# Attention operands kept in three parts per head, a re-ordered first pair of heads, and unread products on TensorE at three stage borders

## The reference, cut to what matters

```python
x = _layernorm(x + attn0(x))    # 16 heads of 8, causal, ALiBi-like decay -|i-j|
x = _layernorm(x + moe(x))      # 8 experts, top 1, 128 -> 512 -> 128
x = _layernorm(x + attn1(x))    # 16 heads of 64, q and k RMS-normalised, gated decay
x = _layernorm(x + ffn(x))      # 128 -> 512 -> 512 -> 512 -> 128
```

## Time and profile before

| | us |
|---|---|
| median of 3 runs | 2205.83 |
| lowest and highest run | 2204.80 and 2212.89 |
| profiled execution, its own time | 2213.37 |
| span of the profile | 2211.6 |
| PE busy | 2041.5 |
| DVE busy | 1389.9 |
| ACT busy | 1146.0 |
| POOL busy | 839.6 |

### The profile page before, as it was taken

The page is one execution under the profiler, slowest core; times in us unless marked ns, Lnnn a source line. Parts: engine busy times, 40 slices in busy tenths (PEclk is TensorE's granted clock), DMA queues, the critical chain, the costliest instruction groups (busy, mean ns, idle before and its releaser), DMA issues.

```text
span 2211.6 us, 37667 instructions
## 1 busy us (share of the span) xinstructions
PE 2041.5 (92%) x13392; PEld 1231.1 (56%) x13392; DVE 1389.9 (63%) x3316; ACT 1146.0 (52%) x1859; POOL 839.6 (38%) x544
## 2 busy tenths in 40 slices
PE   5799999998487988896999999999999999999998
PEld 3355455554476544454566666666666665656644
DVE  4788888883632787874677777777777764333311
ACT  2366666666344676782455555555555552232232
POOL 5000000001501445442577777777777772000000
PEclk8799999999589999995899999999999999999999
DMA  5233333113165689897477677767776697433300
GB/s 177 104 128 133 134 130 119 59 54 98 65 188 151 187 268 338 270 287 181 105 180 180 154 177 180 182 161 173 178 182 166 168 223 211 110 86 86 91 5 10
DMA packets 260313, 336.09 MB, mean 152 GB/s; under 512 B 22732, under 2 KB 181756, under 8 KB 259720
## 3 DMA queue, kind: packets, MB, share of 16 engines
q1 hardware_dynamic: 244824, 305.82, 51.6%
q0 software_dynamic: 7664, 24.39, 3.1%
q10 hardware_dynamic: 7640, 3.48, 0.6%
HBM read 193.69 MB, written 122.62 MB: 143 GB/s over the span
## 4 chain that ended last, share of the span: by engine, by line
PE 49%; DMA 2%; SPq 2%; DVE 0%; ACT 0%; issue 0%; DVEq 0%
PE ps L959 11%; PE ps L1296 10%; PE ps L910 7%; PE ps L941 6%; PE ps L942 6%; PE ps L1247 2%; PE ps L947 1%; PE ps L1307 1%; PE ps L922 1%; PE ps L1284 1%; PE ps L1285 1%; SPq L1171 1%; DMA a1QA<-a1QB 1%; DMA a1FQ<-s_q 1%; DMA s_y<-a1raw 0%; DMA fyb<-s_y 0%
## 5 line engine op out<-in xcount | busy, mean ns | idle before, releaser
L1132 POOL TENSOR_TENSOR a1sum<-a1sum,a1prob 128x1024 f32<-128x1024 f32 (+3 forms) x256 | 461.3, 1802 | 101.7 <-ACT a1prob L1075 69.7
L1075 ACT ACTIVATE a1prob<-ps 128x512 f32<-128x512 f32 (+2 forms) x640 | 322.7, 555 | 239.1 <-PE ps L947 206.3
L480 DVE TENSOR_REDUCE a0grid<-ps 128x8 f32<-128x1024 f32 x288 | 346.6, 1222 | 99.4 <-PE ps L350 48.8
L581 ACT ACTIVATE a0prob<-ps 128x1024 f32<-128x1024 f32 x288 | 291.3, 1027 | 159.0 <-PE ps L376 89.2
L1011 DVE CUSTOM_DVE_ANT_0 ps<-ps,c_mask_ij 128x128 f32<-128x128 f32 x496 | 264.6, 551 | 92.0 <-issue 87.7
L959 PE MATMUL ps<-a1prob,a1V 128*64 128x512 f32 (+3 forms) x1536 | 275.5, 501 | 4.9 <-ACT a1prob L1075 4.9
L941 PE MATMUL ps<-a1QA,a1KA 69*128 69x512 f32 (+3 forms) x768 | 272.3, 362 | 4.0 <-DMA a1QA<-a1neg 4.0
L942 PE MATMUL ps<-a1QB,a1KB 128*128 128x512 f32 (+3 forms) x768 | 264.9, 353 | 0.0
L910 PE MATMUL ps<-a1KA,a1QA 68*128 68x128 f32 x744 | 229.4, 385 | 5.0 <-DMA a1KA<-s_g 4.3
L959 PEld LDWEIGHTS ps<-a1prob,a1V 128*64 128x64 f32 x1536 | 103.3, 139 | 174.4 <-issue 140.2
L1014 DVE TENSOR_REDUCE a1mx<-ps 128x1 f32<-128x320 f32 x248 | 146.0, 589 | 60.0 <-PE ps L910 57.2
(11 more groups left out here) (269 smaller groups left out, 3191.7 us busy)
## 6 DMA issues: line engine op xcount, KB each, us to landing
a1FQ<-s_q SPq DMA_DIRECT2D x128, 256.0 KB, 7.8
a1KB<-s_k SPq DMA_DIRECT2D x128, 256.0 KB, 8.6
s_xs<-c_zero POOLq DMA_DIRECT2D x19, 1024.0 KB, 8.9
s_q<-mqkT SPq DMA_DIRECT2D x32, 512.0 KB, 4.0
s_v<-mv SPq DMA_DIRECT2D x32, 512.0 KB, 5.8
s_k<-a1KH SPq DMA_DIRECT2D x32, 512.0 KB, 4.9
s_k<-a1KL SPq DMA_DIRECT2D x32, 512.0 KB, 5.9
a1KA<-s_k SPq DMA_DIRECT2D x64, 256.0 KB
```

The source lines that it names most:

```text
L480: dve.tensor_reduce(grid[g % 2][:, :, a:b + 1:b - a], banks(("max", k)), axis=AX.X, op=ALU.max).then_inc(s1_free, 1)
L581: act.activation(prob[:, :, a:b + 1:b - a, :], banks(("exp", q)), ACT.Exp).then_inc(p_full, 1)
L1075: act.activation(weights_of(g, u)[:, group[0]:group[-1] + 1, off:BANK], both(e, u, group), ACT.Exp).then_inc(weighed, 1)
L1132: pool.tensor_tensor(t[:, :, off:BANK], t[:, :, off:BANK], weights_of(g, u)[:, :, off:BANK], ALU.add).then_inc(summed, 1)
```

## The change

Scratch q0 and k0 hold three parts per head in neighbouring rows (high, high, low for q; high, low, high for k). `store` makes six transfers of 256 KB per chunk instead of four. K and Q of a group are then loaded by two transfers of 48 rows, BQ and BK by four of 24 rows: six per call of `load_first` or `load_second` instead of sixteen. BK of group 0 is loaded from SP, and `load_second` of group 1 is issued after the row of group 0 instead of between the stores.

`pass_time` is a product of the identity with itself into a bank that nobody reads. There are 8 of 512 columns after the totals, 13 of 512 before `*_last` of PE, one of 256 behind each of the 24 first maxima, and one of 512 behind their turning. At `LAST` DVE does 6 maxima instead of 12 before `gates_b`, and the two `aug` turnings lie between maxima 8 and 9 of the line.

In g = 0 of the second attention the maxima of pair 1 begin at unit 4 instead of 2, `split(2, ...)` lies behind the exponentials of units 4 and 6 instead of 0 and 3, `lower(2, 0)` at unit 8 instead of 4, the turn of pair 1 and its row one unit later, and SP issues the gate rows (`load_e`) first and the values (`load_v`) later.

```diff
+def pass_time(nc, const, bank, tiles):
+    ident = const["ident"]
+    nc.tensor.matmul(bank[:, 0:tiles * P], ident[:, :], ident[:, :].unsqueeze(1).to_broadcast([P, tiles, P]), start=True, stop=True)
...
         def still(engine, buf, name, g, done):
-            for h in range(H):
-                part(engine, buf, name, g, h, done)
+            b, k = divmod(g, per)
+            for m in range(PAIR):
+                row, to, n = 3 * dim * (k * H + m * PAIR), base_of(m) + FIRST, 3 * dim * PAIR
+                engine.dma_start(buf[to:to + n, :].bitcast(F32), scr[name][row:row + n, b * seq:(b + 1) * seq]).then_inc(done, 16)
+        def moving(engine, buf, name, g, done):
+            b, k = divmod(g, per)
             for h in range(H):
-                part(engine, buf[:, h % PAIR, :], name, g, h, done)
+                row, to, n = 3 * dim * (k * H + h), base_of(h // PAIR) + FIRST + 3 * (h % PAIR) * dim, 3 * dim
+                engine.dma_start(buf[to:to + n, h % PAIR, :].bitcast(F32), scr[name][row:row + n, b * seq:(b + 1) * seq]).then_inc(done, 16)
...
-                for r, part in enumerate((high, low)):
-                    nc.sync.dma_start(scr[name][r, :, c * CHUNK:(c + 1) * CHUNK], part[c % PARTS3][:, n, :].bitcast(F32)).then_inc(stored[c % PARTS3], 16)
+                rows_of = scr[name].rearrange("(h s d) n -> h s d n", s=3, d=dim)
+                for s, part in enumerate(((high, high, low), (high, low, high))[n]):
+                    nc.sync.dma_start(rows_of[:, s, :, c * CHUNK:(c + 1) * CHUNK], part[c % PARTS3][:, n, :].bitcast(F32)).then_inc(stored[c % PARTS3], 16)
...
             still(sp, Q[0], "q0", 0, loaded1[0])
+            moving(sp, BK[0], "k0", 0, loaded1[0])
...
-                if c == 5:
-                    sp.wait_ge(cleared, 3)
-                    load_second(sp, 1)
...
-            act.wait_ge(cleared_first, 1)
-            batch_stored(act, 0)
-            moving(act, BK[0], "k0", 0, loaded1[0])
...
-    share0 = ([0, 0, 2, 3, 3, 4, 4, 4, 4, 0, 0, 0], [0, 0, 0, 0, 0, 0, 0, 0, 0, 3, 3, 3])
+    share0 = ([0, 0, 0, 0, 4, 5, 5, 5, 5, 0, 0, 0], [0, 0, 0, 0, 0, 0, 0, 0, 0, 0, 4, 5])
...
         def sync_program():
+            load_e(1)
             for h in range(2):
                 copy_high(1, h)
                 load_a(1, h)
-            load_e(1)
             for k in range(PARTS):
                 load_f(2, k)
+            load_v(1)
+            load_e(2)
             for h in range(2):
                 load_a(2, h)
-            load_e(2)
+            load_v(2)
             for k in range(N_K):
                 load_b(2, k)
...
-                    if u == TILES and g + 2 < G:
+                    if u == (TILES if g > 0 else TURN) and g + 2 < G:
                         lower(g + 2, 0)
...
-                    if g + 2 < G and u in (0, 3):
-                        split(g + 2, (0, 3).index(u))
+                    behind = (0, 3) if g > 0 else (4, 6)
+                    if g + 2 < G and u in behind:
+                        split(g + 2, behind.index(u))
...
             pe.matmul(ps[:, 5, 0:experts], ones[:, :], run[steps % 2][:, :], start=True, stop=True).then_inc(totals, 1)
+            for _ in range(8):
+                pass_time(nc, const, ps[:, 6, :], TILES)
...
+            for _ in range(13):
+                pass_time(nc, const, ps[:, 7, :], TILES)
             pe.wait_ge(ye_full, NT)
...
                     job(k)
                     k += 1
+                    if n == LAST and kind == "max":
+                        pass_time(nc, const, ps[:, 0, :], 2)
+                    if n == LAST and kind == "turn":
+                        pass_time(nc, const, ps[:, 0, :], TILES)
```

More of the change, by code:

```diff
@@ L151, in batch_stored @@
             for c in range(b * seq // CHUNK, (b + 1) * seq // CHUNK):
-                engine.wait_ge(stored[c % PARTS3], 16 * 4 * (c // PARTS3 + 1))
+                engine.wait_ge(stored[c % PARTS3], N_STORE * (c // PARTS3 + 1))
         def load_first(engine, g):
@@ L209, in sync_program @@
             batch_stored(sp, 0)
+            sp.wait_ge(cleared_first, 1)
             still(sp, Q[0], "q0", 0, loaded1[0])
+            moving(sp, BK[0], "k0", 0, loaded1[0])
             for c in range(2, chunks):
@@ L230, in sync_program @@
                     load_first(sp, g + 2)
-                if 0 < g and g + 1 < GROUPS:
-                    sp.wait_ge(s2_full, NU * g)
+                if g + 1 < GROUPS:
+                    if g > 0:
+                        sp.wait_ge(s2_full, NU * g)
+                    else:
+                        sp.wait_ge(cleared, 3)
                     load_second(sp, g + 1)
@@ L576, in exponentials @@
                     for r in range(PARTS3):
-                        act.wait_ge(stored[r], 16 * 4 * len(range(r, chunks, PARTS3)))
+                        act.wait_ge(stored[r], N_STORE * len(range(r, chunks, PARTS3)))
                 if g > 0:
@@ L810, in load_e, with load_v @@
             nc.sync.dma_start(KA[b][EXT:EXT + 4, :, :].bitcast(F32), slopes).then_inc(loaded_e[b], 16)
+        def load_v(x):
+            b, (n, m) = x % NB, divmod(x, PAIRS)
+            if x >= NB:
+                nc.sync.wait_ge(valued, unit(x - NB, NU - 1) + 1)
             nc.sync.dma_start(V[b][:, :, :], scr["v1"][n * S:n * S + S, m * P:m * P + P].rearrange("(t p) n -> p t n", p=P)).then_inc(loaded_v[b], 16)
@@ L864, in sync_program @@
                         load_e(g + 2)
+                        load_v(g + 2)
                         for h in range(2):
@@ L1105, in scalar_program @@
                         keep_den(g - 1)
-                    if u == (TURN if g > 0 else TURN + 2) and g + 1 < G:
+                    if u == (TURN if g > 0 else TURN + 3) and g + 1 < G:
                         row(g + 1)
@@ L1990, in middle @@
         assert turn_gates[LAST]
+        AHEAD = 6
         line = []
@@ L2000, in middle @@
                 here.append((("xT", "gate")[n % 12 // 11], n // 12 + 1, 0))
-            here += [("max", k, 0) for k in range(NM // 2)] if n == LAST else []
-            here += [("aug", c, 0) for c in turn_gates.get(n, ())]
-            here += [("max", k, 0) for k in range(NM // 2, NM)] + [("turn", 0, 0)] if n == LAST else []
+            here += [("max", k, 0) for k in range(AHEAD + 2)] if n == LAST else []
+            for k, c in enumerate(turn_gates.get(n, ())):
+                here += [("aug", c, 0)] + ([("max", AHEAD + 2 + k, 0)] if n == LAST else [])
+            here += [("max", k, 0) for k in range(AHEAD + 2 + len(turn_gates[n]), NM)] + [("turn", 0, 0)] if n == LAST else []
             after_item[n] = here
@@ L2195, in tensor_last @@
                     multiply(n)
-                for _ in after_item[n]:
+                for kind, a, _ in after_item[n]:
                     job(k)
                     k += 1
+                    if n == LAST and kind == "max":
+                        pass_time(nc, const, ps[:, 0, :], 2)
+                    if n == LAST and kind == "turn":
+                        pass_time(nc, const, ps[:, 0, :], TILES)
         def pair(n):
@@ L2360, in vector_last @@
                 if n == LAST:
-                    first_maxima(range(NM // 2))
+                    first_maxima(range(AHEAD))
                 for late in (2, 3):
@@ L2364, in vector_last @@
                         gates_b(event_of[EVENTS[n - late][0]])
-            first_maxima(range(NM // 2, NM))
+            first_maxima(range(AHEAD, NM))
             first_row()
```

15 lines of the change are left out of this document (4 added, 11 removed).

## The result

| | before | after |
|---|---|---|
| median of the runs made together, us | 2209.36 (4 runs) | 2185.74 (4 runs) |
| lowest and highest, us | 2204.80, 2215.85 | 2180.34, 2186.84 |
| profiled execution, its own time, us | 2213.37 | 2186.19 |
| span of the profile, us | 2211.6 | 2184.4 |

The ratio is 0.9886, 95% interval 0.9852 to 0.9920: 1.1% faster, clear of 1. The median lies inside the forecast range of 2152 to 2190 us, at its upper end. Repeated in a later session beside 17 runs of the kernel before, the ratio was 0.9906 (0.9887 to 0.9924), 2187.31 against 2207.93 us. So the change gives 21 to 24 us, where the sum promised 40.

The account below looks back on a forecast made before the run. PE was taken to bound the steady stages, with waits and clock falls at the borders. Gains 12 + 2.5 + 4 + 3 + 18.5 = 40 took the profile from 2213.4 to 2173, the median to 2166 us; range 2152 to 2190.

Parts of the forecast that it names:

- The reading of the earlier trace: Whole kernel before: clock at 2.4 GHz nearly everywhere, dips in four places, plus a small dip in slices 12 and 13.
- Layout, 12 us: Start of first attention: three parts per head let scores begin at 77 instead of 89, gaining 12 us.
- rival (c): First attention: the row at 80 us is late as before, behind 3 MB of stores; 2171 us, chance 6 in 100.
- 8 passes, 2.5 us: Routing to experts: passes after the totals raise the clock before the first tile; 2.5 us gained, from -4 to 4.
- 13 passes, 4 us: Experts to projections: passes within idle time halve PE's work from 719 to 728; 4 us gained, 0 if the clock falls.
- First maxima, 3 us: Projections to second attention: passes and earlier gates shorten the first maxima to 20 us instead of 23.2; 3 us gained.
- g = 0, 18.5 us: Start of second attention: the new order takes 36.5 us instead of 55.0, gaining 18.5 us; lower bound 5.7.
- The last line of the sum: Whole kernel: profiled 2213.4 goes to 2173; the runs' median of 2205.83 lies 7.5 lower than that profile, giving 2166 us.
- Rival (a): Borders and g = 0: the clock doesn't hold, passes give 0 at two borders, g = 0 5.7; 2185 us, 16 in 100.
- Rival (b): g = 0 is bound by transfers, 5 MB in 22 us; 8 us late would make 2174 us; chance 9 in 100.
- (d): Borders and first maxima: the passes make PE the bound at the lower clock, 29 us lost; 2217 us, 4 in 100.
- (e): Start of first attention: DVE's chain, not the loads, sets the pace; 0 of 12, 2178 us, chance 6 in 100.

Follow-up runs that it names:

- no_passes_at_all: The changed kernel with none of its 46 passes, layout and orders kept; ratio to the kernel before 0.9895, 2185.94 us.
- longer_passes: The changed kernel with 10 passes instead of 8, 16 instead of 13, and 2 more behind the first turning of x2; ratio to the kernel before 0.9881, 2175.18 us.
- passes_in_first_pair: The changed kernel with two more 512-column passes before the first maximum of pair 1 and of pair 2 in g = 0; ratio to before 0.9879, 2173.71 us.
- all_gaps_passed: The changed kernel with 10 and 16 border passes, two behind x2's first turning, two before pair 1's and pair 2's first maximum; ratio to before 0.9851, 2177.84 us.
- experiment 1: The kernel before with only the three-part layout of the first attention (stores, loads, their order on SP); ratio 0.9946, 2191.96 against 2203.97 us.
- after_again: The changed kernel, unchanged, timed and profiled again in a later session; ratio to the kernel before 0.9906, 2187.31 us.
- before_again: The kernel before, unchanged, profiled a second time beside the changed kernel; ratio 1.0000 (0.9983 to 1.0018).
- old_first_pair: The changed kernel with g = 0 of the second attention turned back to the old order; ratio to the kernel before 0.9943, 2191.30 us.
- experiments 4 and 5: Additions to the changed kernel: passes or later transfers in g = 0 (4), more border passes (5); ratios to before 0.9878 to 0.9899 (4), 0.9881 and 0.9851 (5).
- transfers_later: The changed kernel with pair 2's QA copies issued ahead of FQ of pair 3, V and KB of pair 2 behind; ratio to before 0.9899, 2179.25 us.
- passes_and_later: The changed kernel with both the extra passes in g = 0 and the reordered transfers of pair 2; ratio to the kernel before 0.9878, 2174.39 us.
- experiment 3: Session with the changed kernel without its 46 passes (0.9895), the changed kernel again (0.9906) and the kernel before again (1.0000), ratios to the kernel before.
- experiment 4: The changed kernel with extra passes in g = 0, with later transfers, and with both; ratios to the kernel before 0.9879, 0.9899, 0.9878.

## Why the prediction came out as it did

The sign and the range held; the likeliest time, 2166 us, was 20 us too low (2185.74). The terms for the passes were worth nothing that shows, and the term for g = 0 was more than twice too large. By its steps:

- **The reading of the earlier trace rows** names a small dip in slices 12 and 13; the row has it in slice 12 alone, which no term of the sum uses.
- **Layout, 12 us: right.** 12.0 us measured alone. PE started 6.5 us earlier as worked out, and rival (c), a late row, did not happen: all 32 rows landed in 1.8 to 3.0 us. The row was issued 1.3 us earlier than the 73.6 that the prediction took from DVE's chain. The loads of Q and BK of group 0 ran at 254 to 303 GB/s from 26 to 27.5 us, where those of the kernel before ran at 8 to 156 from 22.5 to 29.5 us. By the Trainium skill's rule in DMA: Bandwidth & Descriptors ("Why a DMA increments its semaphore by 16 and not by 1") more was to be expected of transfers with 24 and 48 outer rows than of those with 2, and the trace agrees.
- **8 passes, 2.5 us: 0.** "Three or four at the lower level and the rest at the upper" was right (9.49 us). That the clock outlives the wait for the first tile and the short wait behind it was wrong in the profile after (2.08 us for the first eight products), and nothing shows in the time without the passes.
- **13 passes, 4 us: 0 at the end.** The working named the condition, "if the clock is still up after 1.7 us of idling and four turnings", and took its better end. The idling was 2.58 us and the clock fell. At the place the passes gave 0.7 us in one profile of the changed kernel and 2.1 in the other against no_passes_at_all, and 2.3 with the gap closed; the term was too large even with the clock up.
- **First maxima, 3 us: 1.7 at the place** (22.88 to 21.17), of which the order alone 0.4 (0.7 in no_passes_at_all), and nothing that shows at the end. PE waited 1.96 us for DVE before the first `aug` turning, and behind that the clock was at 0.50 from 990 to 993.5. Where it stayed at 1.00 throughout (longer_passes, passes_in_first_pair, all_gaps_passed), the stretch took 19.9 to 20.1 us, the forecast 20.
- **g = 0, 18.5 us: 7.1.** This step carries the error, and it failed at both ends. First, the 55.0 us that it subtracts from came from one execution in which the clock came up some 17 us later than in the three other profiles of the old order; their first pair is 8.3 us shorter on average (59.6 against 67.9). The last line of the sum then took the same execution's 7.5 us off again ("the runs' median lies 7.5 lower than that profile") as if they lay in a part that the change leaves alone. Second, g = 0 took 42.2 us instead of the 36.5, which was worked out at the upper clock: the 16 products of values took 5.72 us where at 1009.32 they took 2.38, and waits of 1.79 and 2.02 us for KA and QA came on top.
- **Rival (a)**, the clock doesn't hold, gave 2185 us and is the nearest; its 0 at the borders is shown. That it came so near is in part luck: it keeps 3 us for the first maxima that don't show, and its 5.7 for g = 0 is near the 7.1 by a bound (clock down all through) that did not occur. **Rival (b)**, transfers: their part is there (1.79 and 2.02 us, not 8), but moving 1.5 MB out of the way gave no more than 0.9899 against 0.9906. **(d)** did not happen: taking out passes gains nothing. **(e)** is refuted by experiment 1.

12.0 + 7.1 and nothing for the passes is 19; the medians beside after_again differ by 20.6 and those of the first measurement by 23.6. That the measured time lies in the range is owed to its width: the range allowed for rival (a).

## What to carry to other kernels

Take the size of a stretch that depends on TensorE's clock from several profiles, or from another kernel that shares its program, before multiplying a promise out of it; and where a profiled run is longer than the median, ask whether the excess lies in the very stretch that is to be shortened. Unread products bring the work behind them to full speed only if they reach up to it: with a block that ended 2.58 us early the first four projections took 3.76 us, with three more passes and two behind the first turning 1.96. Even then the place gained little (0.2 to 1.6 us against the changed kernel), since another engine was waited for next. A higher mean clock is no gain by itself when it comes from unread products.

## What the runs showed of the hardware

**The clock falls and stays down with PE busy.** It was at 0.50 from 1018 to 1030 us with PE recorded 2.93 to 3.00 of 3 us busy (after), and it rose at 1031, in the middle of 16 equal products of values (L970, 1026.81 to 1032.46). By the Trainium skill (TensorE: Matmul & The Clock Gate, "Part 1: The HAM clock gate") the gate follows how busy PE has recently been; at the borders the traces agree, in the first pair that alone does not give what was seen. The same program had it come up 21 us after the first score in one profile (before_again) and 38 us after it in another (before).

**A mean clock is no time.** The runs of no_passes_at_all had a mean clock of 0.958 to 0.961 and those of the changed kernel beside it 0.966 to 0.970, with medians 1.4 us apart. Much of that clock stands where there is no work: from 695 to 700 us it was 1.00 in the changed kernel, with PE busy on passes, and 0.50 in no_passes_at_all, with PE idle. Within one kernel it is otherwise. Of the 17 runs of the kernel before in that session, the fastest (2201.55) had 0.957 and the slowest (2215.70) 0.949, and the others mostly follow in that order.

**What one late copy costs.** In the profile of old_first_pair the 29th interval from one pair's den products to the next took 32.44 us; in the twelve profiles without such a wait this interval took 24.9 to 26.7, and nearly all before it 24.6 to 24.7. PE waited once for QA, and the windows show the rest:
```profile
1758.65 1.09 PE L921 MATMUL ps<-a1KA,a1QA 68*128 68x128 f32 x3 [3.39 <-DMA a1QA<-a1QB]
```
```profile
1755.00:1761.00 6.00, 2.61 (x12) 2.16 (x12) 1.32 (x9) 1.08 (x2) 2.34 (x1) 0.78 0.46 104
1761.00:1767.00 6.00, 6.00 (x23) 4.30 (x22) 4.22 (x13) 1.85 (x4) 3.82 (x3) 0.50 0.01 3
```
A wait of 3.39 us cost 5.7 to 7.6, since the clock fell behind it. The profile of no_passes_at_all has the same in the same interval, from 1746 us (2.51 us waited, 30.10 for the interval). It comes with either order of the first pair, in 2 of 14 profiles; how often it falls into the runs without a profile isn't known.

**A stage that changes with the session.** From the first turning of `*_first` (L1590 of the changed kernel) to the totals it took 51.7 us in all four profiles that were measured together in experiments 4 and 5 (passes_in_first_pair, transfers_later, passes_and_later, longer_passes), and 60.5 to 65.9 in all others, of either order. From 3.5 to 6 us of it come back as a longer time from the totals to the first tile (17.1 us instead of 11.2 to 13.6). No run here shows why, and the chip was the same as that of experiment 3; it is the reason why all_gaps_passed, measured beside the changed kernel, carries the argument on the passes and not the medians of experiment 4.
